# Gated group convolution on one core: conv on 64x32 array tiles, column sums by folding, channel norm on another engine, six input slots

## The reference

```
x_n  = (x - mean) / sqrt(var + 1e-5)                      # per group of 16 channels
ch   = 1x1 conv of [mean(gx), max(gx)] over pixels        # per channel
cw   = sigmoid(norm of ch over its single pixel * gn1_w + gn1_b)
hw   = 1x1 convs of the row means and of the column means of gx
sx   = gx * sigmoid(pos_h) * sigmoid(pos_w)
sx   = conv3x3(sx, w_s3), 16 channels to 16, zero padding, + b_s3
sw   = sigmoid(norm of sx per channel over its pixels)
out  = x + gx * cw * sw
```

## Time and profile before

| what | value |
|---|---|
| time before, median of 3 runs | 4297.46 us (4295.59 to 4298.4) |
| the profiled execution | 4296.2 us, its span 4294.3 us |
| PE busy | 4041.4 us, 94% |
| DVE busy | 4018.4 us, 94% |
| ACT busy | 2624.4 us, 61% |
| POOL busy | 1775.4 us, 41% |
| DMA engines, share of the one data queue | 74.7% |

### The profile page before, as it was taken

The page is one execution under the profiler, slowest core; times in us unless marked ns, Lnnn a source line. Parts: engine busy times, 40 slices in busy tenths (PEclk is TensorE's granted clock), DMA queues, the critical chain, the costliest instruction groups (busy, mean ns, idle before and its releaser), DMA issues.

```text
span 4294.3 us, 55492 instructions
## 1 busy us (share of the span) xinstructions
PE 4041.4 (94%) x11016; PEld 1938.2 (45%) x11016; DVE 4018.4 (94%) x2719; ACT 2624.4 (61%) x4354; POOL 1775.4 (41%) x2314
## 2 busy tenths in 40 slices
PE   5999999999999999999999999999999999999997
PEld 2444444444444444444444444444444444444443
DVE  7999999999999999999999999999999999999996
ACT  3566566666665666666656666666666666665665
POOL 3443444444434434443344434344444344434443
PEclk9999999999999999999999999999999999999998
DMA  6777777777777777777777777777777777777775
GB/s 124 163 173 173 172 175 169 175 172 173 172 173 169 177 173 172 175 167 178 172 172 172 172 176 172 171 172 176 168 177 173 172 175 167 177 173 173 171 177 123
DMA packets 1147751, 730.57 MB, mean 170 GB/s; under 512 B 74144, under 2 KB 1122976, under 8 KB 1147552
## 3 DMA queue, kind: packets, MB, share of 16 engines
q1 hardware_dynamic: 1147552, 728.87, 74.7%
HBM read 268.64 MB, written 268.44 MB: 125 GB/s over the span
## 4 chain that ended last, share of the span: by engine, by line
DVE 53%; issue 18%; SPq 11%; DMA 9%; PE 6%; POOL 1%; ACT 1%; DVEq 1%; POOLq 0%; ACTq 0%
DVE sums L560 13%; DVE mx L607 12%; SPq L222 11%; DMA xt<-in_x 9%; DVE sp_buf L524 7%; DVE sums L554 7%; DVE gated L567 7%; DVE sp_buf L527 6%; PE conv_ps L637 5%; POOL rstd L275 1%; ACT sp_buf L416 1%; DVE gate_hr L594 0%; PE pos_ps L637 0%; DVE ch L603 0%; DVE sums_n L545 0%
## 5 line engine op out<-in xcount | busy, mean ns | idle before, releaser
L637 PE MATMUL conv_ps<-gated,W_conv 128*128 128x512 f32 x6144 | 2973.1, 619 | 16.5 <-DVE gated L567 16.3
L637 PEld LDWEIGHTS conv_ps<-gated,W_conv 128*128 128x128 f32 x6144 | 1143.4, 197 | 1100.0 <-issue 1071.7
L637 PE MATMUL conv_ps<-halo,W_halo 96*128 96x512 f32 x2048 | 1027.7, 604 | 2.1 <-DMA halo<-gated 1.6
L370 ACT ACTIVATE sp_buf<-conv_ps,weights 128x1024 f32<-128x1024 f32 x512 | 565.3, 1104 | 747.8 <-PE conv_ps L637 747.5
L323 POOL TENSOR_TENSOR gated<-gate_w,gate_hr 128x2048 f32<-128x2048 f32 x256 | 918.7, 3609 | 166.9 <-DVE gate_hr L594 157.6
L560 DVE TENSOR_REDUCE sums<-xt 128x128 f32<-128x2048 f32 x256 | 943.6, 3725 | 0.0
L554 DVE TENSOR_REDUCE sums<-xt 128x16 f32<-128x2048 f32 x256 | 584.2, 2282 | 171.5 <-DMA xt<-in_x 171.4
L524 DVE SCALAR_TENSOR_TENSOR sp_buf<-xt,negm,sp_buf 128x2048 f32<-128x2048 f32 x256 | 600.6, 2346 | 38.3 <-ACT sp_buf L416 38.3
L527 DVE SCALAR_TENSOR_TENSOR sp_buf<-sp_buf,kfac,xt 128x2048 f32<-128x2048 f32 x256 | 602.1, 2352 | 9.0
L567 DVE SCALAR_TENSOR_TENSOR gated<-xt,negm,gated 128x2048 f32<-128x2048 f32 x256 | 593.9, 2361 | 0.0
L343 POOL TENSOR_TENSOR rstd<-var_e,consts 128x2 f32<-128x2 f32 x128 | 89.8, 701 | 1176.8 <-DVE var_e L581 1176.8
(11 more groups left out here) (79 smaller groups left out, 2174.4 us busy)
## 6 DMA issues: line engine op xcount, KB each, us to landing
xt<-in_x SPq DMA_DIRECT2D x2048, 128.0 KB, 3.0
out<-sp_buf SPq DMA_DIRECT2D x2048, 128.0 KB, 2.5
halo<-gated SPq DMA_DIRECT2D x512, 365.2 KB, 6.0
weights<-in_by_channel SPq DMA_DIRECT2D x1, 116.5 KB, 2.6
S_chan<-in_same_channel SPq DMA_DIRECT2D x1, 64.0 KB, 1.9
whalo_in<-in_wconv SPq DMA_DIRECT2D x2, 3.0 KB, 1.8
masks<-in_row_masks SPq DMA_DIRECT2D x1, 12.0 KB, 1.9
hmask<-in_halo_mask SPq DMA_DIRECT2D x1, 3.0 KB, 1.9
```

The source lines that it names most:

```text
L370: nc.scalar.activation(sp_buf[:, g, k * 8:k * 8 + 8], conv_ps[:, h % 2], ACT.Identity, bias=V["b_s3"], accum_out=ssum2[:, g, k:k + 1]).the ...
L637: return nc.tensor.matmul(ps, lhsT, rhs, start=start, stop=stop)
```

## The change

1. **Partition order.** Partition = 32 * (row pair) + 2 * channel + (row mod 2). A group of 32 partitions now holds two neighbouring image rows of all channels, and a 3x3 conv of two rows needs only the 64 partitions above and the 64 below.
2. **Conv.** `halo`, its DMAs and its matmuls are gone. Each bank of 512 columns is made by matmuls of 64 partitions by 32 outputs: 4 column tiles from partitions 0 to 63 and 4 from 64 to 127, for each of 3 shifts. The lower halves run one bank behind the upper ones. In all 192 matmuls of 512 columns a unit. `conv_ps` is four banks, and ACT evacuates each bank by itself (8 a unit of 512 columns, before 4 of 1024).
3. **Column sums.** DVE adds block 0..7 to 8..15 (1024 elements), then 0..3 to 4..7 (512), and PE sums the remaining four with the position weights; the means enter as matmuls with `W_rows_m`, `W_cols_m`, `W_ch_m`. `sums_n` and `ch` on DVE and the inputs on POOL are gone.
4. **Channel norm** is six small ACT operations after `cw_ps` and three before `cgate`; its inverse root is in the two added columns of POOL's `rstd` of the next unit.
5. **Order.** DVE: two-input folds and output operations first, then row sums and maximum behind `gate_hr`; POOL's second gate product comes after `kfac`. `xt` has six slots, loads are issued five units ahead, the loop has six bodies.

The first lines of the diff below are POOL's.

```diff
             def body(t, q, k):
+                if real(a):
+                    pool.wait_ge(var_done, a + 1)
+                    if real(t):
+                        pool.wait_ge(ch_var, 6 * t + 6)
...
+                    nc.gpsimd.tensor_tensor(rstd[:, sa], var_e[:, sa % 2], consts[:, 0:4],
+                                            ALU.pow).then_inc(rstd_done, 1)
...
             def evacuate(u, s, n):
-                nc.scalar.activation(sp_buf[:, g, k * 8:k * 8 + 8], conv_ps[:, h % 2], ACT.Identity,
+                nc.scalar.activation(sp_buf[:, g, k * BB:(k + 1) * BB], conv_ps[:, k], ACT.Identity,
                                      bias=V["b_s3"], accum_out=ssum2[:, g, k:k + 1]).then_inc(evac, 1)
...
+            def channel_variance(u, s):
+                act.wait_ge(ch_mm, u + 1)
...
+                for j in range(2):
+                    nc.scalar.activation(ch[:, 0, j:j + 1], cw_ps[:, j:j + 1], ACT.Identity,
+                                         scale=rstd[:, s, j:j + 1], bias=V["b_cc"]).then_inc(ch_var, 1)
...
+            def fold_columns(u, s, j, come):
...
+                nc.vector.tensor_tensor(fold8[:], xt[:, s, j, 0:8], xt[:, s, j, 8:16],
+                                        ALU.add).then_inc(fold8_done, 1)
...
+                nc.vector.tensor_tensor(fold4[:, s % 2, j], fold8[:, 0:4], fold8[:, 4:8],
+                                        ALU.add).then_inc(fold4_done, 1)
...
+                def tiles(u, d, n, half, kw, start):
+                    j, k = n // BANKS, n % BANKS
+                    for o in range(PAIRS):
...
+                        rows = slice(ROW_TILE * half, ROW_TILE * (half + 1))
+                        cols = slice(QUAD * o, QUAD * (o + 1))
+                        ins = mm(conv_ps[cols, k], W_conv[rows, kw, cols],
+                                 gated[rows, d, j, band:band + BB, kw:kw + W], start=start and kw == 0,
+                                 stop=not start and kw == KW - 1)
+                    return ins
```

More of the change, by code:

```diff
@@ L118, in conv_attention @@
         x_in = [[sem(f"x_in{s}{j}") for j in range(2)] for s in range(XS)]
-        halo_in = [[sem(f"halo_in{s}{j}") for j in range(2)] for s in range(2)]
         stored = [sem(f"stored{s}") for s in range(4)]
@@ new lines, in gates @@
+            def gates(u, s):
+                d = s % 2
+                pos = pos_ps[:, 0:2 * (NB + W)].rearrange("p (j n) -> p j n", j=2)
+                act.wait_ge(pos_mm, u + 1)
+                act.wait_ge(rstd_done, u + 1)
+                for j in range(2):
+                    nc.scalar.activation(gate_h[:, d, j], pos[:, j, 0:NB], ACT.Sigmoid,
+                                         scale=rstd[:, s, j:j + 1], bias=b_pos[:, 0:1]).then_inc(gates_done, 1)
+                if later(u, 2):
+                    act.wait_ge(gp_done, 2 * (u - 1))
+                for j in range(2):
+                    nc.scalar.activation(gate_w[:, d, j], pos[:, j, NB:NB + W], ACT.Sigmoid,
+                                         scale=rstd[:, s, j:j + 1], bias=b_pos[:, 1:2]).then_inc(gates_done, 1)
@@ new lines, in channel_gate @@
+            def channel_gate(u, s):
+                act.wait_ge(rstd_done, u + 2)
+                for j in range(2):
+                    nc.scalar.activation(ch[:, 3, j:j + 1], ch[:, 1, j:j + 1], ACT.Copy,
+                                         scale=rstd[:, (s + 1) % XS, 2 + j:3 + j]).then_inc(ch_norm, 1)
+                act.wait_ge(ch_norm, 2 * u + 2)
+                if later(u, 2):
+                    act.wait_ge(kfac_done, u - 1)
+                nc.scalar.activation(cgate[:, s % 2], ch[:, 3], ACT.Sigmoid, scale=V["gn1_w"],
+                                     bias=V["gn1_b"]).then_inc(cgate_done, 1)
@@ L438, in body @@
+                    square1(a, sa, 1, loads(k, q, 1))
+                if real(t):
+                    evacuate(t, q, 0)
+                if real(a):
+                    gates(a, sa)
+                if real(t):
+                    evacuate(t, q, 1)
                 if real(b):
@@ new lines, in positions @@
+                        mm(pos[:, :, 0:NB], W_rows[:, :], sums[:, da], stop=False)
+                        mm(pos[:, :, 0:NB], W_rows_m[:, :], shift.to_broadcast([P, 2, NB]), start=False)
+                        for i in range(4):
+                            mm(pos[:, :, NB:NB + W], W_cols[:, :], fold4[:, da, :, i], start=i == 0, stop=False)
+                        mm(pos[:, :, NB:NB + W], W_cols_m[:, :], shift.to_broadcast([P, 2, W]),
+                           start=False).then_inc(pos_mm, 1)
@@ new lines, in slot @@
+                def slot(n, first=0, last=KW):
+                    if real(t) and first == 0:
+                        if n % BANKS == 0:
+                            pe.wait_ge(mod_done, 2 * t + n // BANKS + 1)
+                        if later(8 * t + n, BANKS):
+                            pe.wait_ge(evac, 8 * t + n - BANKS + 1)
+                        pe.sem_inc(bank_free, 1)
+                    for kw in range(first, last):
+                        if real(t):
+                            ins = tiles(t, q % 2, n, 0, kw, True)
+                            if kw == KW - 1:
+                                ins.then_inc(upper_mm, 1)
+                        if real(t) if n > 0 else real(b):
+                            if kw == 0:
+                                pe.wait_ge(upper_mm, 8 * t + n)
+                                pe.sem_inc(upper_ready, 1)
+                            if n > 0:
+                                ins = tiles(t, q % 2, n - 1, 1, kw, False)
+                            else:
+                                ins = tiles(b, sb_ % 2, 7, 1, kw, False)
+                            if kw == KW - 1:
+                                ins.then_inc(conv_mm, 1)
```

552 lines of the change are left out of this document (248 added, 304 removed).

## The result

The changed kernel takes 4377.0 us (median of four runs, 4365.8 to 4381.6), the kernel before 4296.5. The ratio is 1.018 [1.016, 1.021]: 1.8% slower. The forecast was 4122 us and faster. Its range, 3740 to 4560, holds the time, but its direction was wrong.

What follows compares the result with a forecast made beforehand. It took PE, closely followed by DVE, to bound the kernel before. For the changed one, a 30.6 us loop plus 0.9 for PE's clock gave 31.5 us a turn; 120 + 127 x 31.5 = 4120, plus 1.9: 4122 us, range 3740 to 4560.

Steps and rivals of the forecast that it cites:

- PE first: Kernel before: PE and DVE both near the bound, PE first, its convolution taking 27.5 us of a 32.6 us turn.
- held `rstd`: POOL's 4-column `rstd` waits 2.35 us for DVE's two-input `add_x`; DVE then idles 2.3 us a turn.
- PE's work: PE needs 25.6 to 27.9 us a turn, the convolution taking 48 steps of 0.43 = 20.6 us.
- rival of incomplete overlap: PE's conv tiles overlap incompletely; slower than before from a slot of 3.2 us, 4600 us at 3.5; chance 0.15.
- Halves in a queue: A tile's second matmul record holds back the next tile on PE: 87.6 us a turn, 11200 us; chance 0.12.
- The loop: Chain from `var_e` through POOL, ACT and PE to the next `var_e` decides: 4.6 + 21.4 + 4.6 = 30.6 us.
- The first leg: From DVE's `var_e` through POOL's `rstd` to the end of ACT's gates: 4.6 us.
- I take the first, as only one `rstd` of the two is exposed: ACT's leg taken as 21.4 of 21.4 to 22.6 us; second `rstd` wait 0.7, not 1.9.
- I take half: Half of the up to 1.7 us of PE's work lost to its clock behind a gap: 0.9 us a turn.
- The looser loop: The hold on `rstd` doesn't happen or phases avoid it: 28.7 us a turn, 3765 us; chance 0.24.
- Nothing gained: Clock falls for all of PE's leg, held `rstd` comes twice: 33 us a turn, 4310 us; forecast's upper end.
- The forecast's upper bound: Turn of at most 33.4 us, with array changes and clock in full and the held `rstd`.

Runs made afterwards that it cites:

- e12: Kernel before with the middle column shift of its convolution left out, a quarter of its conv records; 4294.4 us, 1.000 of before.
- e1: Changed kernel with DVE's `add_x` moved ahead of the maxima and `var_e`, one-input work in its old place; 4163.0 us, 0.970.
- e15: Changed kernel with one wait added: DVE starts `add_x` only when POOL's `rstd` is done, all orders unchanged; 4165.2 us, 0.970.
- e3: Changed kernel with the edits of e1 and e2 together; 3936.7 us, 0.917.
- e14: Changed kernel with the edit of e2 plus the DVE wait of e15; 3830.8 us, 0.891.
- e4: Changed kernel with three matmuls whose result nobody reads added ahead of `gn_ps`, where PE waits for ACT; 4227.7 us, 0.984.
- e5: Changed kernel with one unused ACT operation of 1.06 us added ahead of the first spatial sigmoid; 4276.3 us, 0.996.
- e2: Changed kernel with PE's `gn_ps` for the second group moved behind `positions`, the last tiles and `norm_ps`; 3945.3 us, 0.919.

## Why the prediction was wrong, point by point

- **What bounds the kernel before: "PE first" was wrong.** e12 shows that PE did not bound it. What is left is DVE with its 31.4 us of work and 1.3 of waiting for loads: in the middle of the span it waits for nothing else but 0.1 us a turn for ACT. That reading rests on the trace; no run made DVE's work smaller in the kernel before and nothing else. Two engines at 94% were ordered by comparing conv time with turn time, where leaving work out was needed. The forecast's sum didn't use this step, but it made a lighter PE look like a gain by itself.
- **DVE: right.** 3473.7 / 128 = 27.1 us of work (27.6 forecast), folds 1.22 and 0.69 (1.28 and 0.69), no wait for `xt`. The held `rstd` came as worked out: 2.92 us, `gate_hr` 4.75 us behind `var_e` (4.7), DVE idle 2.32 (2.3). e1 and e15 show its price, 1.7 us a turn. The Trainium skill (SBUF — State Buffer, Who interferes with whom) has the exclusion that these rows show; its reverse side, a DVE operation held by POOL's, is the 2.16 us in e3.
- **PE's work: at its upper end, and for another reason.** At the full clock PE is busy for 27.9 us in e14's turn, where 25.6 to 27.9 were forecast. The price of a step was right: eight records start within 0.05 us, and the next eight 0.43 us later. What was wrong is the count. In the turn of the changed kernel the 384 records come in 52 steps and not in 48, because eight of them hold only four records. A whole step and a half-filled one, as windows that count every record running in them (eight of the step before and eight new ones; eight and four):

```profile
2036.03:2036.46 0.43, 0.43 (x16) 0.15 (x8) 0.43 (x1) 0.43 (x3) 0.43 (x1) 1.00 1.07 211
...
2037.33:2037.69 0.36, 0.36 (x12) 0.14 (x5) 0.36 (x1) 0.36 (x1) 0.00 (x0) 1.00 0.36 64
```

  The half-filled steps stand mostly at the ends of stretches and once within each pair of slots; what makes them was not tried. Two slots take 5.67 us instead of 5.1, and the convolution of e14's turn 22.5 instead of 20.6. That is most of the way from 25.6 to 27.9 and leaves at most 0.4 us for the changes between tiles and the full array, to which the forecast had given up to 2.3. A slot of 2.84 us is under the 3.2 at which the rival of incomplete overlap decides.
- **Halves in a queue: fell.** 96 records take 5.67 us, where 48 matmuls at 0.43 would take 20.6. The Trainium skill (TensorE: Matmul & The Clock Gate, The mechanism) says that matmuls start and end in program order; what these rows refute is the step that the rival built on it, that a tile's second record holds back the next tile. The rows don't name the tile of a record, so how the two records of one matmul lie to each other stays open.
- **The loop: right as a mechanism, under-sized in two terms.** The first leg was 4.60 (4.6 forecast). Without any loss of clock the sum was 30.6 us, and turns at the full clock last 31.7. The difference is all in ACT's leg, and there in the wait for the second `rstd`: "I take the first, as only one `rstd` of the two is exposed" is the step that failed. ACT's leg was given as 21.4 to 22.6 and is 22.6 in a usual turn; ACT waits 2.33 us for this `rstd`, where 0.7 stood in the sum (the channel operations gave 0.5 of that back, 2.2 for 2.7). It is held in 121 of 122 turns, for 2.13 us on average. "The hold depends on phase" left open what could be read from the new order, in which `gate_x` is under way when POOL is asked. The second failed step is "I take half", 0.9 us for the clock. PE's leg is 4.50 with the gap filled (e4; 4.6 forecast) and 6.07 without, 1.6 us more: the slow stretch starts with the work behind the gap, and that work is the leg. Over all turns, with more than one slow stretch in some, the clock costs 33.5 - 31.7 = 1.8 us. Together 1.1 + 0.9 = 2.0 us a turn, which is 31.5 against 33.47; outside the turns 124 us answer 120.
- **And a wrong reason behind a right number.** ACT's passes add up to less than their leg. In the middle the loop runs over DVE and the second hold (e5, where 1.0 us of added work on ACT left the second `scale` within 0.2 us of where it was). Trimming ACT there, which the forecast suggests, should buy nothing; that was not run.
- **The looser loop: fell as the result, but it is near what the kernel could do.** It was priced at 28.7 us a turn and 3765 us, for the case that the hold doesn't happen. e14 takes the first hold and the PE gap away: its usual turn is 28.5 us and its time 3830.8, as one turn of six is longer.
- **"Nothing gained", 33 us and 4310 us, was the nearest of the cases, and its price was added up wrongly.** By its own terms, the whole 1.7 us of clock and the second hold of 1.2, it is 30.6 + 1.7 + 1.2 = 33.5 us and 4376 us, which is what was measured. The forecast's upper bound has the same slip: with changes of the array, clock and hold all in full the sum gives 4.6 + 22.6 + 5.2 + 1.7 = 34.1 us, not 33.4, or 4450 us: the measured 4377 lie outside its 3960 to 4360, but inside what its own terms allowed. The break-even was at (4297 - 122) / 127 = 32.9 us, well inside the bounds: both signs were open, and a chance of 0.36 within 0.42 for faster was too much.

Where the expected gain went: the 4.3 us a turn that DVE was relieved of became its own idle time, 3.8 ahead of `var_e` and 2.3 ahead of `gate_hr`, because the loop was longer than either engine's work.

## What to carry to other kernels

When every engine gets lighter, look for the chain that closes on itself, add it up from one turn's timeline, and ask of each link what stands in front of it in its engine's order; here one matmul asked for too early (10 points of the ratio, e2) and one operation started too early (5 points, e1 and e15) decided the sign of the whole change. Lay turns of different length side by side and see which column differs; here it was the granted clock alone. To learn whether an engine is the bound, leave a part of its work out: with PE at 94% and at 88%, neither kernel got faster when a quarter or a third of the convolution's records was gone. And choose a term's value by its position in the new order, not by splitting the difference between its bounds, and add up each bound anew from its terms.
